# Graph kernel on one core: GpSimd waits for the landing of four gathers in the middle of each group of eight

## The chip, the cores and the metric

The kernel runs on one core of a Trainium2 chip. The metric is the device time of one execution in microseconds. Three runs of the kernel before gave 9080.73, 9087.52 and 9103.37 us; the median is 9087.52 us.

## What is computed

One node array x of 6250 rows by 256 goes through two layers. Each has a graph part and a mixture of experts part, all in float32. The reference, cut to its core:

```python
edge_index = jnp.stack([src, dst])          # 206250 edges, sorted by dst
x = x + _L0_gnn_ref(_layernorm(x, axis=-1), edge_index, ...)       # attention, 4 heads
x = x + _L0_ffn_ref(_layernorm(x, axis=-1)[None], ...)[0]          # 8 experts, top 2
x = x + _L1_gnn_ref(_layernorm(x, axis=-1), src, dst, edge_weight, ...)
x = x + _L1_ffn_ref(_layernorm(x, axis=-1)[None], ..., edge_index)[0]  # 4 experts

# in _L0_gnn_ref
e = jax.nn.leaky_relu(a_src[src] + a_dst[dst], negative_slope=NEG_SLOPE)
...
out = jax.ops.segment_sum(alpha[:, :, None] * h[src], dst, num_segments=N)

# in _L1_gnn_ref
messages = edge_val[:, None] * embeddings[edge_src]
neighbor_emb = jax.ops.segment_sum(messages, edge_dst, num_segments=embeddings.shape[0])
```

Both graph parts have the same skeleton: for every edge the row of its source node is fetched, scaled, and added to the sum of its destination node.

## The kernel before, in words

The 206250 sorted edges are cut into tiles of 128. `graph_pass` (L693) runs twice, once per graph part. Fetching the 128 source rows of a tile is one gather, an indirect DMA that GpSimd issues from a table in HBM to `G`, 128 rows of 1040 bytes in pass 1 and of 1024 bytes in pass 2. Gathers come in groups of `GRP` = 8, and `G` is a ring of `RINGS` = 4 groups. Each ring place r has its own semaphore `gather_done[r]`, which each gather raises by 16 when it has landed, 128 for a whole group.

**Pass 1** (`attend`, 208 groups, 1664 gathers, L831). GpSimd waits at the start of group k until the last pair of sums of group k - 4 is done, since it will write into the same ring place, and then issues eight gathers with nothing between them. The consumers of group k are:

- VectorE waits for `gather_done` (L789), forms the attention argument (`g_Z` L987, `g_L`, `g_ARG` L998), multiplies the rows by the factors in four products (L981), builds one-hot matrices (`g_S` L921) and adds the sums out of PSUM into `acc` (L944).
- ScalarE takes the exponentials (L1064, L1065) and copies the turned one-hots out of PSUM (`g_ST` L1048).
- TensorE turns the one-hots (L1095), spreads node values to edges (`g_pA` L1105) and sums messages by destination, two tiles to a pair and four pairs to a group (`g_pM` L1115). Each pair raises the semaphore `part` by one. ScalarE's copy, VectorE's adds and its `g_Z`, and GpSimd's next group all wait on values of `part`.

In step k TensorE's order is: turns for k + 1, pairs 2 and 3 of group k - 1, pair 0 of group k, the spread for k + 1, pair 1 of group k. From round 1 to round 50 of 52, VectorE and ScalarE also do a piece of a sort of other edges in every second group (L897 and L903, or L1052 and L1056). After the last group GpSimd issues 16 small scatters of that sort (L618).

**Pass 2** (202 groups, 1616 gathers, L839). A slot of work may straddle two groups, so ScalarE waits for the landed counts and raises `tiles` (L1040, L1041), TensorE waits on `tiles` and forms the sums (L1147) in two halves, each raising `sum`. VectorE builds one-hots times weight (L932) and adds to `acc` (L952), one of each in turn. SyncE waits for a number of `sum` from a table (L819) and raises `room`; GpSimd waits on `room` before group g, at most three groups ahead of what was consumed. In the last 130 groups one scatter (L618) follows the eight gathers.

Each engine's instructions are written out in program order in its own block; nothing is reordered. GpSimd has one instruction queue, so all that it issues stands in the order shown. The two steps in question, as they stand:

```python
if k >= RINGS:
    pool.wait_ge(s["part"], summed(k - RINGS, PAIRS - 1))      # pass 1
...
at_least(pool, s["room"], g - AHEAD + 1)                       # pass 2
```

`rounds0` is 0 for pass 1 and 52 for pass 2, the number of times that each ring place was filled before.

Of the kernel before, what the change touches and what calls it, by code (L numbers as in the profile page):

```python
# [47 lines left out]
GRP = 8  # L48
RINGS = 4
# [97 lines left out]
def at_least(eng, sem, value):  # L147

    if not isinstance(value, int) or value > 0:
        eng.wait_ge(sem, value)  # L150
# [542 lines left out]
def graph_pass(sh, tag, planned, planned_block, table, width, acc, acc_zeroed, gather_done, rounds0, keep=None, gmax=None,  # L693
# [11 lines left out]
    HG = GRP // 2  # L705
# [9 lines left out]
    with Scope(nc) as sc:  # L715
# [81 lines left out]
        def summed(k, pair):  # L797
            return k * PAIRS + 5 + pair
# [5 lines left out]
        @block.sync  # L804
        def _(sp):
            sp.dma_start(IDX[:, :], planned[0] if attend else src_tiles).then_inc(s["loaded"], 16)
            sp.dma_start(REL[:, :], planned[1]).then_inc(s["loaded"], 16)
            if attend:
                sp.dma_start(BLK[:, :], planned_block).then_inc(s["loaded"], 16)
            if ranking:  # L810
                sp.dma_start(DST, sort.dst_t).then_inc(s["loaded"], 16)
                sp.dma_start(SRC, sort.src_t).then_inc(s["loaded"], 16)
            if not attend:
                sp.dma_start(WT[:, :], planned[2]).then_inc(s["loaded"], 16)

                with sp.Fori(0, TG - AHEAD) as g:
                    sums = sp.value_load(tables.summed(g), min_val=1, max_val=2 * SG)
                    sp.wait_ge(s["sum"], sums)
                    sp.sem_inc(s["room"], 1)  # L819

        @block.gpsimd
        def _(pool):
            pool.wait_ge(s["loaded"], n_loads)

            def step_attending(k):

                r = k % RINGS
                if k >= RINGS:
                    pool.wait_ge(s["part"], summed(k - RINGS, PAIRS - 1))
                for u in range(GRP):  # L830
                    pool.indirect_dma_start(G[:, r, u, :], None, table, bass.IndirectOffsetOnAxis(  # L831
                        ap=IDX[:, k * GRP + u:k * GRP + u + 1].bitcast(U32), axis=0)).then_inc(gather_done[r], 16)

            def step_placing(g):

                r = g % RINGS
                at_least(pool, s["room"], g - AHEAD + 1)
                for u in range(GRP):
                    pool.indirect_dma_start(G[:, r, u, :], None, table, bass.IndirectOffsetOnAxis(  # L839
                        ap=IDX[:, g * GRP + u:g * GRP + u + 1].bitcast(U32), axis=0)).then_inc(gather_done[r], 16)  # L840
                if g >= TG - place:
                    sort.place(pool, 1)

            if attend:
                pool.iota(RANK, [[P, NTF]], base=P * NTS, channel_multiplier=1,
                          allow_small_or_imprecise_dtypes=True).then_inc(s["rank0"], 1)
                for k in range(SG):
                    step_attending(k)
                pool.wait_ge(s["prep"], 7)
                pool.wait_ge(s["addr"], 4)  # L850
                sort.place(pool, tail)
            else:
                for g in range(TG):
                    step_placing(g)
                sort.place(pool, tail)
# [1859 lines left out]
```

## Time and profile before

| | |
|---|---|
| median of 3 runs | 9087.52 us (9080.73 to 9103.37) |
| span of the profiled execution, first to last instruction | 9073.9 us |
| the profiled execution's own time | not listed apart; the median lies 13.6 us above its span |
| busy share: PE, DVE, ACT, POOL | 64%, 43%, 17%, 60% |
| gathers of pass 1, first to last start | 202.7 to 2756.2 us |
| gathers of pass 2, first to last start | 4301.8 to 6845.9 us |
| granted TensorE clock, mean | 0.756 |

The profile is of one execution. PE is TensorE, DVE is VectorE, ACT is ScalarE, POOL is GpSimd, SP is SyncE. A timeline row gives start, duration, engine, line, operation, output and inputs; in brackets stands the idle time of the engine before it and what ended it. "issue" there means that the engine waited for nothing the profile shows, "remote" that the releaser was found on no recorded instruction. An indirect DMA's busy time on POOL is the making of its descriptors, not the transfer.

### The profile page before, as it was taken

Reading aid. Unit: us, or ns where it says so; the run is one execution under the profiler, and the core shown is the slowest. Engines: PE = TensorE matmul, PEld = TensorE weight load, DVE = VectorE, ACT = ScalarE, POOL = GpSimd, SP = SyncE. Lnnn points to the kernel's source line nnn. Section 1 sums busy time; section 2 is a strip of 40 time slices with the busy share of each in tenths; the row PEclk is TensorE's granted clock in tenths of the full one; section 3 lists DMA queues with packets and bytes.
Section 4 is the critical chain, followed back from the end, with each engine's and each line's share of the span. In section 5 each row is a group of like instructions: output and inputs, shape, how many; then the busy total and the mean of one; then the engine's idle time right before and its main releaser. Section 6 shows DMA issues by size and latency. Waiting matters only on the chain. (4 is left out here: it accounts for less than half of the span.)

```text
span 9073.9 us, 116515 instructions
## 1 busy us (share of the span) xinstructions
PE 5819.2 (64%) x27644; PEld 4894.5 (54%) x27645; DVE 3938.2 (43%) x10109; ACT 1583.2 (17%) x3574; POOL 5476.3 (60%) x5690
## 2 busy tenths in 40 slices
PE   4677777777772488881444444444442579998984
PEld 3566665666662477771333333333331478888883
DVE  4566666777776400004444434434331532222225
ACT  1122222221220233330000000000000233333331
POOL 3566666666666466666666666666666246666662
PEclk7777777777775599995777777776765768888786
DMA  3333333333333144443333222222220022222345
GB/s 113 84 88 87 89 89 85 88 86 87 87 86 108 49 140 145 145 145 114 88 89 88 86 81 81 81 80 82 79 82 19 22 60 67 65 69 65 67 67 163
DMA packets 426058, 793.32 MB, mean 87 GB/s; under 512 B 129162, under 2 KB 267134, under 8 KB 425684
## 3 DMA queue, kind: packets, MB, share of 16 engines
q0 software_dynamic: 235504, 474.87, 21.0%
q1 hardware_dynamic: 190436, 317.20, 10.4%
q14 instruction: 84, 0.69, 0.0%
q8 instruction: 34, 0.56, 0.0%
HBM read 720.67 MB, written 70.98 MB: 87 GB/s over the span
## 5 line engine op out<-in xcount | busy, mean ns | idle before, releaser
L1147 PE MATMUL g_pM<-g_G,g_S 128*128 x3328 | 1178.4, 531 | 1570.5 <-DVE g_S L932 834.9
L831 POOL DMA_INDIRECT g_G<-table,X x1664 | 1620.8, 974 | 933.8 <-issue 447.1
L839 POOL DMA_INDIRECT g_G<-table,g_IDX x1616 | 1534.2, 949 | 863.9 <-issue 460.8
L1147 PEld LDWEIGHTS g_pM<-g_G,g_S 128*128 128x128 f32 x3328 | 903.1, 278 | 1845.8 <-issue 1652.9
L1115 PE MATMUL g_pM<-g_G,g_S 128*128 128x260 f32 x3328 | 1196.4, 499 | 593.1 <-DVE acc L944 555.7
L1691 POOL DMA_INDIRECT q_G<-table,slot x1072 | 1037.1, 967 | 591.5 <-issue 288.3
L618 POOL DMA_INDIRECT slots<-sort_PAIR,sort_ADDR x1024 | 1012.3, 989 | 521.4 <-issue 310.7
L952 DVE TENSOR_TENSOR acc<-g_pM,acc 128x256 f32 x1664 | 697.2, 419 | 1257.4 <-remote 693.1
L1115 PEld LDWEIGHTS g_pM<-g_G,g_S 128*128 128x128 f32 x3328 | 722.3, 238 | 906.4 <-DVE acc L944 647.2
L944 DVE TENSOR_TENSOR acc<-g_pM,acc 128x260 f32 x1664 | 711.4, 428 | 468.4 <-remote 204.0
L932 DVE TENSOR_SCALAR g_S<-iota,g_REL,g_WT 128x128 f32<-128x128 f32 x1664 | 588.8, 354 | 288.2 <-issue 259.2
L1105 PEld LDWEIGHTS g_pA<-keep,g_ST 128*128 128x128 f32 x3328 | 555.1, 257 | 80.7 <-issue 69.0
L1477 PE MATMUL q_pH<-ew_XT,ew_W 128*128 (+1 forms) x3136 | 552.6, 347 | 52.9 <-ACT ew_GT L1496 34.6
L1105 PE MATMUL g_pA<-keep,g_ST 128*128 x3328 | 550.1, 297 | 11.9 <-ACT g_ST L1048 1.2
L1477 PEld LDWEIGHTS q_pH<-ew_XT,ew_W 128*128 128x128 f32 x3136 | 514.4, 254 | 71.7 <-ACT ew_GT L1496 42.3
L981 DVE TENSOR_TENSOR g_G<-g_G,g_pF 128x512 f32<-128x512 f32 x832 | 546.6, 678 | 0.3 <-issue 0.3
L1351 ACT ACTIVATE f_XT<-f_pT 128x512 f32<-128x512 f32 x49 | 28.9, 596 | 2804.9 <-issue 2640.8
L2372 PE MATMUL e_pH<-e_XT,e_W 128*128 128x128 f32 x3360 | 410.9, 282 | 164.4 <-ACT e_XT L2316 155.3
L2372 PEld LDWEIGHTS e_pH<-e_XT,e_W 128*128 128x128 f32 x3360 | 391.9, 195 | 204.9 <-ACT e_GT L2333 178.7
L2350 DVE TENSOR_TENSOR e_Y<-e_pY,ew_B 128x256 f32<-128x256 f32 x105 | 44.6, 425 | 924.8 <-PE e_pY L2381 895.2
L1487 PE MATMUL q_pY<-ew_W,ew_GT 128*128 128x256 f32 x1568 | 435.9, 428 | 0.0
L2381 PE MATMUL e_pY<-ew_W,e_GT 128*128 x1680 | 380.3, 379 | 0.7 <-DVE e_Y L2350 0.7
(335 smaller groups left out, 7007.3 us busy)
## 6 DMA issues: line engine op xcount, KB each, us to landing
e_W<-in_L_ffn_W SPq DMA_DIRECT2D x210, 512.0 KB
sort_PAIR<-slot_rows SPq DMA_DIRECT2D x66, 512.0 KB
g_G<-table,X POOLq DMA_INDIRECT x1664
g_G<-table,g_IDX POOLq DMA_INDIRECT x1616
ys_all<-ew_Y SPq DMA_DIRECT2D x196, 128.0 KB
sm_Y<-ys_all SPq DMA_DIRECT2D x28, 896.0 KB, 10.5
q_ST<-slot_rows SPq DMA_DIRECT2D x34, 512.0 KB
sort_ADDR<-slot_rows SPq DMA_DIRECT2D x34, 512.0 KB
```

The costliest lines, as they stand in the source:

```text
L618: pool.indirect_dma_start(self.slots, bass.IndirectOffsetOnAxis(ap=self.ADDR[:, t:t + 1].bitcast(U32), axis=0), self.PAIR[:, t, :], None). ...
L831: pool.indirect_dma_start(G[:, r, u, :], None, table, bass.IndirectOffsetOnAxis(ap=IDX[:, k * GRP + u:k * GRP + u + 1].bitcast(U32), axis= ...
L839: pool.indirect_dma_start(G[:, r, u, :], None, table, bass.IndirectOffsetOnAxis(ap=IDX[:, g * GRP + u:g * GRP + u + 1].bitcast(U32), axis= ...
L932: v.tensor_scalar(S[:, r, u, :], sh.iota[:, :], rel, WT[:, bass.ds(k * GRP + u, 1)], ALU.is_equal, ALU.mult).then_inc(s["onehot"], 1)
L944: v.tensor_tensor(node_sums(blk), pM[u % BANKS][:, 0:width], node_sums(blk), ALU.add).then_inc(s["added"], 1)
L952: v.tensor_tensor(node_sums(blk), pM[r % 2 * 2 + u // HG][:, u % HG, :], node_sums(blk), ALU.add).then_inc(s["added"], 1)
L1105: m = pe.matmul(pA[:, r % 2, u, :], ST[:, u, :], nodes, start=True, stop=True)
L1115: m = pe.matmul(pM[u % BANKS][:, 0:width], S[:, r, u, :], G[:, r, u, :], start=True, stop=True)
L1147: m = pe.matmul(pM[r % 2 * 2 + half][:, u % HG, :], S[:, r, u, :], rows.rearrange("p a d -> p (a d)"), start=True, stop=True)
L1477: m = pe.matmul(self.pH[e % n][:, c, :], self.W1[:, e, k, c * P:(c + 1) * P], self.XT[:, bass.ds(i, 1), k, :].rearrange("p a m -> p (a m)" ...
L1691: pool.indirect_dma_start(G[:, r, u, :], None, table, bass.IndirectOffsetOnAxis(ap=node_of_slot[:, 2 * (k * GRP + u):2 * (k * GRP + u) + 1 ...
L2372: m = pe.matmul(pH[j % 2][:, c, :], W1[:, j, k, c * P:(c + 1) * P], XT[:, j % 2, k, :], start=(k == 0), stop=(k == KC - 1))
```

## The change

Behind the fourth gather of each group, in both passes, GpSimd now waits on the semaphore of the group's ring place until the 64 increments of these four gathers have arrived on top of all those of earlier rounds. `HG` is `GRP // 2` = 4. Nothing else is changed, and no instruction is moved.

```diff
@@ step_attending(k), pass 1
                 for u in range(GRP):
                     pool.indirect_dma_start(G[:, r, u, :], None, table, bass.IndirectOffsetOnAxis(
                         ap=IDX[:, k * GRP + u:k * GRP + u + 1].bitcast(U32), axis=0)).then_inc(gather_done[r], 16)
+                    if u == HG - 1:
+                        pool.wait_ge(gather_done[r], (k // RINGS + rounds0) * 16 * GRP + 16 * HG)
@@ step_placing(g), pass 2
                 for u in range(GRP):
                     pool.indirect_dma_start(G[:, r, u, :], None, table, bass.IndirectOffsetOnAxis(
                         ap=IDX[:, g * GRP + u:g * GRP + u + 1].bitcast(U32), axis=0)).then_inc(gather_done[r], 16)
+                    if u == HG - 1:
+                        pool.wait_ge(gather_done[r], (g // RINGS + rounds0) * 16 * GRP + 16 * HG)
                 if g >= TG - place:
                     sort.place(pool, 1)
```

## Rows read from the trace of the kernel before

**Rows 1.** The page, part 1: busy time and share of each engine.

```profile
PE 5819.2 (64%) x27644; PEld 4894.5 (54%) x27645; DVE 3938.2 (43%) x10109; ACT 1583.2 (17%) x3574; POOL 5476.3 (60%) x5690
```

**Rows 2.** Busy time in two windows, pass 1 and pass 2, in the page's order.

```profile
202.70:2757.10 2554.40, 1968.97 (x8236) 1543.45 (x8236) 1711.90 (x3607) 506.88 (x869) 1620.78 (x1664) 0.76 0.32 87
4301.80:6846.90 2545.10, 1168.07 (x3296) 895.12 (x3296) 1034.05 (x3295) 0.00 (x0) 1662.28 (x1745) 0.71 0.29 83
```

**Rows 3.** Waits of POOL in pass 1: us in total, times, longest.

```profile
POOL g_G L831 <- issue: 447.1, 1460, 0.5
POOL g_G L831 <- PE g_pM L1115: 363.7, 143, 10.9
POOL g_G L831 <- remote: 122.9, 61, 2.1
```

**Rows 4.** Waits of POOL in pass 2, the same columns.

```profile
POOL g_G L839 <- issue: 460.8, 1505, 1.3
POOL g_G L839 <- SPq L819: 382.7, 110, 11.5
POOL slots L618 <- issue: 39.3, 129, 0.3
```

**Rows 5.** Line L831: who waited for its gathers (us, times), the whole answer.

```profile
who waited for it (us, times):
  DVE g_Z L987: 7.6, 1
```

**Rows 6.** Timeline of POOL in pass 1: first and eighth gather of a group, next starts.

```profile
904.89 0.94 POOL L831 DMA_INDIRECT g_G<-table,X  x1 [2.77 <-PE g_pM L1115]
...
913.64 0.95 POOL L831 DMA_INDIRECT g_G<-table,X  x1 [0.30 <-issue]
...
916.62 0.94 POOL L831 DMA_INDIRECT g_G<-table,X  x1 [2.03 <-PE g_pM L1115]
...
929.48 0.94 POOL L831 DMA_INDIRECT g_G<-table,X  x1 [3.17 <-PE g_pM L1115]
```

**Rows 7.** The other engines at the end of that group.

```profile
912.20 3.24 PE L1115 MATMUL g_pM<-g_G,g_S 128*128 128x260 f32 x8 [2.05 <-DVE acc L944]
...
916.32 1.02 ACT L1048 ACTIVATE g_ST<-g_pT 128x1024 f32<-128x1024 f32 x1 [4.27 <-PE g_pM L1115]
916.52 1.00 DVE L944 TENSOR_TENSOR acc<-g_pM,acc 128x260 f32 x2 [2.64 <-PE g_pM L1115]
```

**Rows 8.** Timeline of the start of pass 1, 32 gathers without a wait.

```profile
211.54 0.95 POOL L831 DMA_INDIRECT g_G<-table,X  x1 [0.30 <-issue]
...
214.41 0.19 DVE L987 TENSOR_TENSOR g_Z<-g_G,g_pA 128x32 f32<-128x32 f32 x1 [7.65 <-DMA g_G<-table,X]
...
221.49 2.08 PE L1115 MATMUL g_pM<-g_G,g_S 128*128 128x260 f32 x4
...
241.54 0.95 POOL L831 DMA_INDIRECT g_G<-table,X  x1 [0.30 <-issue]
...
247.66 0.19 DVE L987 TENSOR_TENSOR g_Z<-g_G,g_pA 128x32 f32<-128x32 f32 x1 [27.89 <-remote]
```

**Rows 9.** Timeline of pass 2, two groups of gathers with two scatters.

```profile
5405.08 0.97 POOL L839 DMA_INDIRECT g_G<-table,g_IDX  x1 [3.40 <-SPq L819]
...
5414.88 0.33 DVE L932 TENSOR_SCALAR g_S<-iota,g_REL,g_WT 128x128 f32<-128x128 f32 x1
...
5429.80 0.35 DVE L932 TENSOR_SCALAR g_S<-iota,g_REL,g_WT 128x128 f32<-128x128 f32 x1 [0.97 <-issue]
...
5430.91 0.97 POOL L839 DMA_INDIRECT g_G<-table,g_IDX  x1 [3.44 <-SPq L819]
```

**Rows 10.** Timeline of the end of pass 1; the last of the 16 scatters is first.

```profile
2776.43 0.95 POOL L618 DMA_INDIRECT slots<-sort_PAIR,sort_ADDR  x1 [0.30 <-issue]
...
2781.29 0.19 DVE L987 TENSOR_TENSOR g_Z<-g_G,g_pA 128x32 f32<-128x32 f32 x1 [18.81 <-remote]
...
2790.43 0.19 DVE L987 TENSOR_TENSOR g_Z<-g_G,g_pA 128x32 f32<-128x32 f32 x1 [1.34 <-PE g_pM L1115]
```

## The prediction

> **What bounds the kernel now.** I read busy shares first, then the two passes by window, then who waits for whom, then single groups in time. The shares name no engine: PE has 64%, POOL 60% [rows 1]. The passes are 5100 of 9074 us, and in them POOL issues 1664 gathers in 2554 us and 1616 gathers plus 129 scatters in 2545 us, with no other engine above 1970 us busy [rows 2]. So the question is how POOL's time per group is made up.
>
> A gather costs POOL 0.95 us (mean 0.974 in pass 1) and 0.306 us of issue behind it (447.1 / 1460) [rows 2, 3], so gathers start 1.25 us apart. Eight are 10.0 us. A group takes more: 11.7 us from 904.89 to 916.62 and 12.9 us to 929.48 [rows 6]. The rest is the wait at the group's start, 204 waits in pass 1 with 486.6 us in all, mean 2.39 [rows 3], and 110 in pass 2 with 382.7 us, mean 3.48 [rows 4]. In pass 2 only every second group waits: from 5405.08 to 5430.91 eighteen indirect DMAs stand in one stream [rows 9].
>
> Nobody waits for the gathers' data: one wait of 7.6 us, the first of the pass [rows 5]. So the ring is full, POOL waits for its consumers, and a landing is needed by nobody for two groups.
>
> But these consumers are not simply slow. At 912.20 PE starts pairs 2 and 3 of a group. By the row it is done at 915.44 for both, so the first pair should be free some 1.5 us earlier, yet ScalarE's copy and VectorE's add, which wait for that first pair alone, start at 916.32 and 916.52 [rows 7]. The eighth gather had ended issuing at 914.59 (913.64 + 0.95) [rows 6], so this is 1.7 to 1.9 us after the end of issue. How long after issue do gathers land? The very first group says it: the eighth gather ends issuing at 212.49, and `g_Z`, which waits only for the landing, starts at 214.41, 1.92 us later [rows 8]. The consumers go on just as the gathers in flight have landed. At the pass's start this is plain: 32 gathers run without a wait until 242.49. The pair sums that PE finishes at 223.57 free `g_Z` of the next group, whose rows have landed long ago, and it starts at 247.66 [rows 8]. That is 24 us held, and released only after the stream has stopped. At the end of the pass the 16 scatters do the same: VectorE idles 18.8 us until their stream is over, and then does a whole group in 9.1 us (2781.29 to 2790.43) [rows 10]. In pass 2, one-hots follow at once early in a stream and with 0.97 us of "issue" between them late in it [rows 9].
>
> My reading: **news from PE, and late in a long stream the other engines' instructions too, are held up while GpSimd streams indirect DMAs, and are let go when those in flight have landed.** The present boundary wait is a lock: POOL waits for a pair sum, and that is held until POOL has been still for about 2 us.
>
> **The change part by part.** It adds 208 + 202 = 410 waits and removes nothing. Queued behind each on POOL are the group's gathers 5 to 8, in late pass 2 one scatter, and then the next group's boundary wait.
>
> *A mid wait.* No row has this wait, so it is bounded. Below: 1.92 us from end of issue to a consumer's start [rows 8]. Above: 3.44 us, the wait behind a stream of eighteen [rows 9]. I take 2.05: its stream is eight gathers long, and the waits behind such a stream are 2.03 [rows 6] and "remote" 122.9 / 61 = 2.01 [rows 3]. It replaces one issue gap of 0.306, so it adds 1.744 us, 410 times: 208 x 1.744 = 363 us and 202 x 1.744 = 352 us.
>
> The Trainium skill, DMA: Bandwidth & Descriptors, Anatomy of one DMA, gives 2.0 us plus bytes / 436e3 for a GpSimd DMA, setup included. An estimate by it is 2.3 us from issue for 133 KB, thus 1.36 us of waiting behind the 0.95 us, and the sum would be 410 x 0.69 = 283 us less than mine. The trace has 2.87 us for this length (211.54 to 214.41) and decides [rows 8].
>
> *The boundary wait.* It hides the mid wait if it goes away. Between two mid waits stand again eight gathers (four of this group, four of the next), so once per period everything held is let go. PE's pair sum that the boundary asks for is four groups old; consumers need 9.1 us for a group when let run [rows 10], the new period is 10.0 + 1.74 = 11.8 us, so they draw ahead until they wait for data. Then the boundary costs nothing: pass 1 loses its excess of 486.6 - 204 x 0.306 = 424 us, pass 2 its 382.7 - 110 x 0.306 = 349 us. A few remain where consumers do extra work, of up to 10.9 us [rows 3] and 11.5 us [rows 4]; I leave 12 us in pass 1 and 12 us in pass 2.
>
> *Ends of the passes.* At the end of pass 1 consumers now have over two groups left, held behind the scatters and done at 9.1 us each [rows 10]. With consumers ahead, one group less is left: 9 us, in pass 2 about 6 us (a bit less work per group). What is late next is the landing of gathers 5 to 8, which `g_Z` waits for.
>
> **Sum.** Pass 1: 363 - 424 + 12 - 9 = -58. Pass 2: 352 - 349 + 12 - 6 = +9. Together -49 us against the profiled span: 9073.9 - 49 = 9025. The median stands 13.6 us above that span, so 9038. In pass 2 nearly nothing is won, since one wait of 3.5 per two groups is traded for two of 2.05; in pass 1 one of 2.39 for one of 2.05.
>
> All other work (projections, experts, slot pass) is untouched.
>
> **Rivals.** (a) *The boundary waits stay and the mid waits come on top.* POOL is on the path, a landing is exposed, and 410 x 1.744 = 715 us are added: 9800 us. The mechanism: POOL's period grows from 11.7 to 13.5 us and the pair sum is still not told when POOL comes to the boundary. It decides from the point where over one group in seven keeps a second stop (49 / 1.744 = 28 groups of 208 in pass 1 cancel the gain; 44 of them lose 0.3%). For it: groups with a sorting piece run late, the wait before 929.48 is 3.17 us [rows 6], and one that misses the mid stop may be held for a whole period. Against it: each second stop lets the consumers go twice in a period, and they have 13.5 us for 9.1 us of work, so they catch up and the second stop goes. A share of a third of the groups, 70 + 67 stops of 1.744 = 239 us above the sum, is the most I can believe: 9277 us. The Trainium skill's rule for overlap (DMA: Bandwidth & Descriptors, Rules for kernel authors) says to issue early and wait on the semaphore late; by it this rival would be the whole story.
>
> (b) *Nothing changes within 0.3%* (27 us, about what a measurement of this kernel can tell). The limit is how fast held news can be passed on, so that a group needs 12.2 us however the stops are cut, or the mid wait is 2.2 us instead of 2.05 (410 x 0.15 = 61 us more) and eats the gain. For it: pass 1 and pass 2 take the same time per group today, 12.3 and 12.6 us, with quite different work. 9087, range 9060 to 9115.
>
> (c) *A larger gain.* The mid wait is at its lower bound 1.92 (-53 us), no long waits remain (-24), and both pass ends give back what stream stops hide today (another -20): 8941 us. For it: the 24 us stall at the start of pass 1 and the 18.8 us at its end [rows 8, 10].
>
> (d) *The wait does nothing*, because the four gathers have landed when POOL comes to it. Excluded: POOL comes to it at the end of issue of the fourth, 1.92 us too early.
>
> **How the numbers follow.** The forecast with its own range 8990 to 9060 has 0.45, (c) 0.13, (b) 0.22, (a) 0.20, mostly in its mild form. The likeliest time is 9038. The range runs from (c)'s middle, 8965, to 9180, which takes in 54 groups in both passes that keep a second stop above (b)'s 9087 (93 / 1.744); about 0.05 is left out below and 0.12 above. Faster by over 0.3%: 0.45 + 0.13 = 0.58. Within: 0.22. Slower: 0.20.
>
> **What the changed profile would show.** Right: before the fifth gather of every group POOL idles about 2.05 us, released by the gather's own DMA, 410 times; the waits of POOL on PE L1115 and on SyncE's L819 fall from 487 and 383 us to some tens; the first gather to the last takes about 2504 us in pass 1 and 2560 us in pass 2; `g_Z` now waits for DMA; VectorE in pass 2 runs at its early pace nearly throughout. ScalarE's copy in pass 1 starts about 1.8 us after the fourth gather's end of issue instead of the eighth's. Wrong: waits on PE L1115 remain about 200 in number (rival a), or the mid wait is 2.2 us or more (b). If the mid wait leaves held news held, my reading of the lock is wrong as a whole, and the time lies above 9180.

## The result, and the profile after

The changed kernel takes 8955.41 us (median of 3 runs, 8952.56 to 8956.40) against 9087.52 us: a ratio of 0.9854 with a 95% interval of 0.9836 to 0.9871, 132 us less. I had forecast 49 us less, 9038 us, with a range down to 8965. The direction and the exchange of waits hold, the size does not. The profiled execution has a span of 8954.6 us against 9073.9 us, 119.3 us less. The other 13 us are spread between executions: in every run on record the time is 1.7 to 2.1 us above the span of the same execution, so the profiled execution of before took about 9076 us, less than any of the three timed ones, while the profiled one of after took 8956.4 us, 1 us above the median.

First the page, part 1, of the changed kernel, and its row for line L831 (busy us, mean ns, then idle time in front of it and what ended most of it).

```profile
PE 5685.7 (63%) x27644; PEld 4815.9 (54%) x27645; DVE 3949.8 (44%) x10109; ACT 1585.0 (18%) x3574; POOL 5436.7 (61%) x5690
...
L831 POOL DMA_INDIRECT g_G<-table,X x1664 | 1576.4, 947 | 876.9 <-DMA g_G<-table,X 433.4
```

The shares again name nobody. Then the two passes by window, in the page's order of engines, each from its first to the end of its last gather:

```profile
210.40:2663.60 2453.20, 1800.73 (x8279) 1440.60 (x8280) 1729.86 (x3628) 509.53 (x873) 1576.42 (x1664) 0.80 0.33 90
4193.00:6743.00 2550.00, 1208.62 (x3312) 925.12 (x3312) 1038.60 (x3320) 0.00 (x0) 1663.93 (x1745) 0.71 0.28 83
```

Pass 1 is 101 us shorter, pass 2 is 5 us longer [rows 2]. The granted TensorE clock of pass 1 is 0.80 instead of 0.76 in these rows; POOL does not wait for PE in this pass any more, and no run separates what part the clock has in that. And POOL's waits (us in total, times, longest), first in pass 1, then in pass 2:

```profile
POOL g_G L831 <- DMA g_G<-table,X: 433.4, 208, 2.8
POOL g_G L831 <- issue: 428.2, 1406, 0.3
...
POOL g_G L831 <- PE g_pM L1119: 15.2, 50, 0.3
```

```profile
POOL g_G L841 <- issue: 433.6, 1414, 3.1
POOL g_G L841 <- DMA g_G<-table,g_IDX: 412.8, 201, 2.4
POOL slots L618 <- issue: 39.9, 131, 0.3
```

This is the exchange that was forecast, and it is complete on this chip. The mid wait is there 208 and 201 times, 2.08 and 2.05 us each (the 202nd, 3.1 us, stands under "issue"). The waits at the group boundary, 486.6 us in pass 1 [rows 3] and 382.7 us in pass 2 [rows 4], are gone to the last: the 50 that still name PE last 0.30 us each, as an ordinary issue gap does, and SyncE, whose count released them in pass 2, is named no more. POOL's time in pass 1 now adds up without a rest: 1576.4 + 428.2 + 15.2 + 433.4 = 2453.2 us.

The timeline of one group in pass 1 (start, duration, engine, line, operation; in brackets the idle time before):

```profile
906.66 0.95 POOL L831 DMA_INDIRECT g_G<-table,X  x1 [0.30 <-PE g_pM L1119]
...
910.42 0.95 POOL L831 DMA_INDIRECT g_G<-table,X  x1 [0.30 <-issue]
...
912.98 0.19 DVE L991 TENSOR_TENSOR g_Z<-g_G,g_pA 128x32 f32<-128x32 f32 x1 [3.10 <-remote]
...
913.41 0.95 POOL L831 DMA_INDIRECT g_G<-table,X  x1 [2.05 <-DMA g_G<-table,X]
...
918.42 0.95 POOL L831 DMA_INDIRECT g_G<-table,X  x1 [0.30 <-issue]
```

From 906.66 to 918.42 the group takes 11.76 us, where before it took 11.7 to 12.9 [rows 6]. `g_Z`, for which VectorE had been idle, starts 1.6 us after the fourth gather's end of issue (911.37): the consumers are let go in the middle of the group now. The trace also holds the times at which semaphores rise, and "news from PE" here is a rise of `part`. Over gathers 200 to 1650, PE's first news in each of the 181 mid stops comes 1.74 us (median) after the fourth gather's end of issue (5% to 95%: 1.64 to 1.81); before, it came 1.72 us (median) after the eighth's. An example from before: the pairs whose matmuls end at 913.63 and 915.44 by their rows raise `part` at 916.30 and 916.36. Not all news in a stream is held: in the kernel before, the next rise of `part` follows the end of a pair by 0.01 us (median of 88) when the pair ends in the first 2 us of a stream, and by 3.75 us (median of 80) when it ends 6 to 8 us into it.

Pass 2, two groups with a scatter in each:

```profile
5309.88 0.94 POOL L841 DMA_INDIRECT g_G<-table,g_IDX  x1 [2.04 <-DMA g_G<-table,g_IDX]
...
5312.50 0.35 DVE L936 TENSOR_SCALAR g_S<-iota,g_REL,g_WT 128x128 f32<-128x128 f32 x1 [0.67 <-issue]
...
5337.07 0.94 POOL L841 DMA_INDIRECT g_G<-table,g_IDX  x1 [2.07 <-DMA g_G<-table,g_IDX]
```

Where a stream of eighteen ran between two waits [rows 9], there is now a stop in each nine. And the end of pass 1:

```profile
2658.90 0.94 POOL L831 DMA_INDIRECT g_G<-table,X  x1 [2.51 <-DMA g_G<-table,X]
...
2673.76 0.19 DVE L991 TENSOR_TENSOR g_Z<-g_G,g_pA 128x32 f32<-128x32 f32 x1 [8.59 <-remote]
...
2695.20 0.36 DVE L1206 TENSOR_TENSOR f_Z<-keep 128x196 f32<-128x196 f32 x1 [0.53 <-PEq L135]
```

VectorE is held for 8.6 us behind the sixteen scatters, not for 18.8 [rows 10], and the work behind the pass (`f_Z`) starts 32.6 us after the last gather's start, not 46.3.

Stage by stage, the spans differ by: start of pass 1 +7.7 us (POOL waits 80.6 us for the load of `fsrc`, not 71.7; kernels with the same code there show 71 to 81), pass 1 -101.3, its end -13.7, between the passes -1.2, pass 2 +4.8, its end -6.8, the stage behind it -8.4, the rest -0.3. Sum -119.2.

**A part that was not in the forecast.** Gathers in pass 1 last 947 ns in the mean, not 974 [rows 2]: 44.4 us of POOL's busy time. The rows show which. Before, where VectorE ranks for the sort:

```profile
1528.38 2.34 DVE L897 TENSOR_TENSOR_SCAN X<-g_pF,g_BASE,X 128x1024 f32<-128x1024 f32 x1
...
1529.87 0.94 POOL L831 DMA_INDIRECT g_G<-table,X  x1 [0.30 <-issue]
...
1530.89 1.35 DVE L903 COPY_PREDICATED X<-X 128x1024 f32<-128x1024 int32 x1 [0.16 <-DVE X L897]
...
1531.11 1.91 POOL L831 DMA_INDIRECT g_G<-table,X  x1 [0.30 <-issue]
```

The gather beside the predicated copy takes 1.91 us; the gather beside the scan takes 0.94. There are 50 such copies, all of them 6.02 us behind the start of a stream, and 53 gathers above 1.05 us; the 50 beside the copies start 0.21 to 0.40 us into the copy. After, the copy starts 8.7 to 10.1 us behind the stream's start. Sixteen copies stand in no gather, as here:

```profile
1522.83 0.95 POOL L831 DMA_INDIRECT g_G<-table,X  x1 [0.31 <-issue]
...
1524.18 1.36 DVE L907 COPY_PREDICATED X<-X 128x1024 f32<-128x1024 int32 x1 [0.16 <-DVE X L901]
...
1525.82 0.94 POOL L831 DMA_INDIRECT g_G<-table,X  x1 [2.05 <-DMA g_G<-table,X]
```

### The profile page after: what moved, and what is told of

Same layout as the page of the kernel before. It is cut to its first block and busy times, and to the rows that moved or that the text cites. A ratio compares the mean times of both kernels' runs of the same rounds, so it can differ in the third digit from the quotient of the medians.

```text
span 8954.6 us, 116515 instructions
## 1 busy us (share of the span) xinstructions
PE 5685.7 (63%) x27644; PEld 4815.9 (54%) x27645; DVE 3949.8 (44%) x10109; ACT 1585.0 (18%) x3574; POOL 5436.7 (61%) x5690
## 5 line engine op out<-in xcount | busy, mean ns | idle before, releaser
L1151 PE MATMUL g_pM<-g_G,g_S 128*128 x3328 | 1213.9, 543 | 1525.6 <-ACTq L1045 1372.6
L831 POOL DMA_INDIRECT g_G<-table,X x1664 | 1576.4, 947 | 876.9 <-DMA g_G<-table,X 433.4
L1151 PEld LDWEIGHTS g_pM<-g_G,g_S 128*128 128x128 f32 x3328 | 929.2, 287 | 1810.3 <-issue 1608.0
L1119 PE MATMUL g_pM<-g_G,g_S 128*128 128x260 f32 x3328 | 1249.2, 534 | 661.4 <-DVE acc L948 638.4
L1119 PEld LDWEIGHTS g_pM<-g_G,g_S 128*128 128x128 f32 x3328 | 817.7, 263 | 947.6 <-DVE acc L948 726.2
L618 POOL DMA_INDIRECT slots<-sort_PAIR,sort_ADDR x1024 | 1017.5, 994 | 487.1 <-issue 310.6
L1109 PEld LDWEIGHTS g_pA<-keep,g_ST 128*128 128x128 f32 x3328 | 426.6, 202 | 55.1 <-issue 36.9
L1109 PE MATMUL g_pA<-keep,g_ST 128*128 x3328 | 410.0, 255 | 6.1 <-ACT g_ST L1052 1.2
```

The lines of the kernel that those rows point to most:

```text
L618: pool.indirect_dma_start(self.slots, bass.IndirectOffsetOnAxis(ap=self.ADDR[:, t:t + 1].bitcast(U32), axis=0), self.PAIR[:, t, :], None). ...
L1109: m = pe.matmul(pA[:, r % 2, u, :], ST[:, u, :], nodes, start=True, stop=True)
L1119: m = pe.matmul(pM[u % BANKS][:, 0:width], S[:, r, u, :], G[:, r, u, :], start=True, stop=True)
L1151: m = pe.matmul(pM[r % 2 * 2 + half][:, u % HG, :], S[:, r, u, :], rows.rearrange("p a d -> p (a d)"), start=True, stop=True)
```

## The experiments

The chips differ (the kernel before takes 9074 to 9211 us on them), so ratios to the kernel before on the same chip are compared, and stages within one chip where nothing else is said. `no_stop`, at 0.9997, stands for the kernel before where I compare stages on its chip. A profile is of one execution: three traces from one chip with the same code in pass 1 (`pass1_only`, `change_again`, `late_stops16`) have 2492 to 2502 us for it, so a stage is known to about 10 us.

**1. The halves of the change.** The wait of one pass is left out in each.

```diff
 # pass1_only: step_placing without
-                    if u == HG - 1:
-                        pool.wait_ge(gather_done[r], (g // RINGS + rounds0) * 16 * GRP + 16 * HG)
 # pass2_only: step_attending without the same two lines (with k)
```

> The mid wait in pass 1 alone. Lock theory (held news is let go when GpSimd stops for a landing): pass 1 shrinks by about 101 us and its tail by 15, as in the trace of the change, the rest stays: 9087 - 116 = 8971 us. If pass 2 carried half of the gain: 9020 us.

> The mid wait in pass 2 alone. Lock theory: one wait of 3.5 us per two groups is traded for two of 2.06, so the pass itself costs 5 us more and its tail gives 16 back: 9087 - 11 = 9076 us, within 0.3%. If pass 2 carried half of the gain: 9020 us.

Measured: 0.9873 (0.9843 to 0.9903) and 0.9979 (0.9966 to 0.9992). Both came as the lock theory had them (8971 of 9087 is 0.9872, and pass 2 alone within 0.3%). The product is 0.9852, the change 0.9854, so the halves add and nearly all is won in pass 1. By stages against `no_stop`, pass 1 goes from 2606 to 2493 us with its wait, and pass 2 from 2562 to 2552 us with its own, a difference of the size of the spread; the end of pass 2 from 29 to 20 us.

**2. The wait, or the stop?** The wait stays as an instruction in its place, but on the group before, which has landed long ago.

```diff
-                    if u == HG - 1:
-                        pool.wait_ge(gather_done[r], (k // RINGS + rounds0) * 16 * GRP + 16 * HG)
+                    if u == HG - 1 and k > 0:
+                        pool.wait_ge(gather_done[(k - 1) % RINGS], ((k - 1) // RINGS + rounds0 + 1) * 16 * GRP)
```

> The wait stands at the same place, but for the eight gathers of the group before, the last of which was issued 5 us earlier and has landed: GpSimd runs through a wait and does not stop. Lock theory: no stop, nothing is let go, the boundary waits return: 9087 us, same as before. Rival (the wait as such, or fewer gathers that could be in flight, does it): faster by over 50 us.

Measured: 0.9997 (0.9981 to 1.0013). Its waits of POOL in pass 1:

```profile
POOL g_G L831 <- PE g_pM L1119: 472.6, 169, 10.6
POOL g_G L831 <- issue: 447.1, 1460, 0.5
POOL g_G L831 <- remote: 73.3, 35, 2.2
```

All 204 boundary waits are back, 545.9 us (this chip is one of the slower ones). A wait instruction that does not stop POOL does nothing here; the stop is what acts.

**3. Where the stop stands, and how many.**

```diff
 # behind_eighth
-                    if u == HG - 1:
+                    if u == GRP - 1:        # value: the whole group
 # fourth_and_eighth
+                    if u in (HG - 1, GRP - 1):
 # every_second
+                    if u == HG - 1 and k % 2 == 0:
```

> The same wait, but behind the eighth gather, where the boundary wait stands. Streams are again eight long and each group has one stop: if only the number of stops and the length of streams matter, the same time as the change within 0.3%, 1.3% faster than before in pass 1's share, with waits of 2.08 us. If the place matters (a pair sum that comes just behind the stop must wait for the next), the waits on part come back at 0.5 us a group and the gain halves.

> Waits behind the fourth and behind the eighth gather. The boundary needs no second stop, so it is pure cost: 410 x (2.08 - 0.31) = 726 us above the change, 9680 us. If shorter streams (four instead of eight) also sped the consumers so that GpSimd was no longer the bound, it would cost less than 600 us.

> The mid wait in even groups only, so that streams are sixteen gathers long. Lock theory: half the mid waits are saved (205 x 1.78 = 364 us), but news is held for some 10 us of each 22 us; with 9.1 us of work per group the consumers have too little time, boundary waits return, and pass 1 takes as long as before or a little more: 0 to 2% slower than the change. Rival (8 gathers per stop is more than needed): 2 to 4% faster than the change.

Measured: 0.9892 (0.9871 to 0.9913); 1.0615 (1.0583 to 1.0648); 1.0211 (1.0191 to 1.0231). The place is of little weight in the passes: behind the eighth, pass 1 takes 2456 us and pass 2 2556 us, 4 and 7 us more than the change's 2452 and 2549. The whole kernel is 0.4% slower than with the stop behind the fourth, a little outside the 0.3% that was expected; of the 29 us between the spans 16 lie behind the first gather of the slot pass (`q_G`), and why was not settled. A second stop in each group adds its full price, since there is no boundary wait left for it to replace:

```profile
POOL g_G L831 <- DMA g_G<-table,X: 781.6, 374, 2.9
POOL g_G L831 <- issue: 382.2, 1247, 0.5
POOL g_G L831 <- PE g_pM L1119: 85.3, 41, 2.1
```

These are 415 stops of 2.09 us (781.6 + 85.3 over 374 + 41). On the same chip, against the kernels with one stop per group, pass 1 takes 365 us more (2858 against 2493 of `pass1_only`) and pass 2 354 us more (2906 against 2552 of `pass2_only`), together 719 us beside the 726 expected. Over the kernel before the run lies 570 us. A stop in every second group is worse than none: streams of sixteen form, and the 147 boundary waits that are left take 427 us (339.8 + 87.3) beside 217 us of stops. It is 3.6% slower than the change, where 0 to 2% was expected. Rival (a) exists, then, in this kernel and not in the change.

**4. Must POOL wait for the landing?** Iotas into a tile of their own stand in place of the wait. They need no transfer and stop the stream for 0.75, 1.26, 1.77 or 2.27 us (1, 2, 3 or 4 of them).

```diff
-                        pool.wait_ge(gather_done[r], (k // RINGS + rounds0) * 16 * GRP + 16 * HG)
+                        if k > 0:
+                            pool.wait_ge(s["filled"], k * n)
+                        for f in range(n):
+                            pool.iota(FILL[:, f, :], [[1, 512]], base=0, channel_multiplier=0,
+                                      allow_small_or_imprecise_dtypes=True).then_inc(s["filled"], 1)
```

> In place of the wait, GpSimd writes 512 numbers a partition into a scratch buffer (iota, some 0.5 to 0.6 us and one issue gap), so the stream pauses for less than 1 us and no landing is waited for. Lock theory: a pause shorter than the 1.9 us to the landing lets nothing go; the boundary waits stay, partly shortened by the filler's time: between 0 and 3% slower than before. Rival (any pause in descriptor making lets the news through): boundary waits gone, 410 x 1 us less than the change, some 3% faster than before.

> Four such fillers, some 3 to 3.6 us without a new gather and no wait on a landing. Lock theory: the gathers in flight land during them, held news goes, and the boundary waits are gone or nearly so; the pause itself is about 1.3 us longer than the wait of 2.08 us: 410 x 1.3 = 533 us above the change, about 4% slower than before. Rival (the wait on the semaphore itself is what helps): boundary waits of 486 and 383 us stay on top, over 10% slower than before.

> Nothing is left out. In both passes the wait behind the fourth gather is replaced by two iotas of GpSimd into a tile of their own, so the pause between the fourth and the fifth gather is about 1.26 us (0.75 us with one iota, 2.27 us with four, by their runs) and waits for no transfer. Theory 'landing' (news is let go when the gathers in flight have landed, which takes about 1.8 us from the last one's issue): 1.26 us is too short, the boundary waits stay near one iota's (median 1.5 us) or near before's 2.03 us, and the time is 9240 to 9290 us. Theory 'backlog' (the news is worked off during any pause, and a group of eight needs some 1.7 to 2.0 us of pause in all, in one piece or in several): the median boundary wait is near 1.0 us and the time stays near one iota's, 9150 to 9200 us; pass 1 then takes about 2540 us as with no pause and with one iota.

> Nothing is left out. Three iotas in place of the wait: a pause of about 1.77 us (estimate from 0.75 us with one and 2.27 us with four). Both theories allow that the boundary waits go; the point is how much pause is enough. If 1.77 us is enough: 208 pauses in pass 1 and 202 in pass 2, each 0.31 us shorter than the change's 2.08 us, take 127 us off the change's 8955 us: 8830 us, with all boundary waits at 0.30 us. Theory 'landing' with its 1.8 us from issue to landing: just short of it, boundary waits stay in a good part of the groups, 9000 to 9300 us. Theory 'backlog': boundary waits of 0.3 to 0.6 us at most, 8830 to 8950 us.

Measured, with readings of the semaphore events of gathers 200 to 1650 (181 pauses; one can also be without news because PE has none to tell):

| pause, us | ratio (interval) | pauses without news from PE, of 181 | boundary waits of pass 1, us |
|---|---|---|---|
| 0.30 (`no_stop`) | 0.9997 (0.9981 to 1.0013) | not counted | 545.9 |
| 0.75 (`filler1`) | 1.0115 (1.0095 to 1.0135) | 164 | 400.7 |
| 1.26 (`filler2`) | 1.0248 (1.0206 to 1.0291) | 117 | 608.7 |
| 1.77 (`filler3`) | 1.0037 (1.0023 to 1.0051) | 87 | 283.2 |
| 2.27 (`filler4`) | 1.0005 (0.9996 to 1.0015) | none | 62.1 (0.30 each) |
| 2.08 (the change) | 0.9854 (0.9836 to 0.9871) | none | 62.2 (0.30 each) |

The rows come from chips on which the kernel before takes 9205 us (`no_stop`), 9211 us (`filler2`, `filler3`) and 9081 to 9088 us (the others; 486.6 us of boundary waits in the kernel before there, not 545.9). Read by pass, the table is not one curve. With one iota pass 1 takes 2541 us, about as before (2553), and all of the loss is in pass 2, 2662 us instead of 2544. With two it is the other way round: pass 1 takes 2832 us (2606 in `no_stop`), pass 2 2562 us, the same as in `no_stop`. POOL's waits on PE in pass 1 with two, three and four iotas:

```profile
POOL g_G L832 <- PE g_pM L1128: 579.0, 125, 8.3
```

```profile
POOL g_G L832 <- PE g_pM L1128: 258.9, 128, 6.6
```

```profile
POOL g_G L832 <- PE g_pM L1128: 28.0, 92, 0.3
```

A pause of 2.27 us with no wait on a transfer clears the boundary as the wait does. Its time is the change's plus the longer pause: 208 x 0.19 + 202 x 0.28 (means 2.27 and 2.34 against 2.08 and 2.06) = 96 us of the 119 us between their spans. (The 4% that was expected came from a pause of 3 to 3.6 us; the four iotas took 2.27.) With a pause of 1.77 us about half of the groups get no news, and this is best seen in time (three iotas, two groups):

```profile
1003.65 1.60 POOL L838 IOTA g_FILL<- 128x512 f32 x3
...
1004.66 0.19 DVE L1000 TENSOR_TENSOR g_Z<-g_G,g_pA 128x32 f32<-128x32 f32 x1 [2.14 <-remote]
...
1015.15 1.59 POOL L838 IOTA g_FILL<- 128x512 f32 x3
...
1016.91 0.96 POOL L832 DMA_INDIRECT g_G<-table,X  x1 [0.16 <-issue]
...
1019.07 0.19 DVE L1000 TENSOR_TENSOR g_Z<-g_G,g_pA 128x32 f32<-128x32 f32 x1 [5.58 <-remote]
...
1024.84 0.95 POOL L832 DMA_INDIRECT g_G<-table,X  x1 [3.21 <-PE g_pM L1128]
```

The first pause lets `g_Z` start; in the second nothing starts, VectorE idles 5.58 us, and POOL pays 3.21 us at the boundary. The boundary waits of this run mostly alternate in the first half of the pass, 0.3 and 2.1 to 3.4 us. With two iotas it is worse. VectorE (its waits from 500 to 2500 us) is held for up to 9.4 us. My reading, not shown apart, is that PE's sums are then really late, not only told late; POOL's waits for them sum to more than with no iota:

```profile
DVE g_Z L1000 <- remote: 500.6, 93, 9.4
```

Neither theory of `filler2` and `filler3` is right as a whole. "Backlog" had them at 9150 to 9200 and 8830 to 8950 us; by their ratios, on a chip with 9081 us for the kernel before, they take 9306 and 9115 us. "Landing" had 9240 to 9290 and 9000 to 9300, so it is nearer. But with one iota the news at the boundary came 1.28 us (median) after the end of issue, before the last transfer's end, which is at 1.48 us in this kernel as in the four others where I read it (before, after, two and three iotas). It came 0.44 us earlier than before's 1.72, about what the iota had lengthened the mid pause by (0.45 us). So the last transfer's end is not what lets the news go, though it comes near in time. Nor is there one delay: where news comes in a pause of two or three iotas, it comes 0.99 and 1.00 us (medians) after the end of issue, not 1.74 as in the change or 1.73 as with four iotas. Some pauses without news had nothing to tell (by the ends of the pairs some 15 of the 87 with three iotas). What lets the news go was not settled; shown is that a pause of 2.08 us let news out 181 times in 181, and one of 1.77 us in about half.

**5. The copies beside the gathers.** The predicated copy is cut to 16 of its 1024 columns, in the kernel before and in the changed one. Both kernels leave out most ranks of the sorted edges with it, so the second expert layer works on other data.

```diff
-                v.copy_predicated(RANK, EQ[j].bitcast(I32), SCAN).then_inc(s["rank"], 1)
+                v.copy_predicated(RANK[:, 0:16], EQ[j].bitcast(I32)[:, 0:16], SCAN[:, 0:16]).then_inc(s["rank"], 1)
```

> The kernel before with VectorE's predicated copies of the sort (50 of 1.35 us, L903) cut to 16 of 1024 columns, so the ranks of the sorted edges are left out and the second expert layer's graph is not the reference's. The trace of before shows 50 gathers of about 1.9 instead of 0.95 us beside these copies. If these 47 us were on the path: about 50 us faster than before (0.5%), gathers at 0.947 us mean. If the boundary wait swallows them: under 15 us.

> The changed kernel with the same cut copies. Its gathers are at 0.947 us already, GpSimd is the bound and not VectorE: within 10 us of the change. Rival (VectorE's load in sorting groups still counts): 30 to 60 us faster than the change.

Measured: 1.0016 (1.0003 to 1.0030) and 0.9918 (0.9902 to 0.9935). In the kernel before the gathers of pass 1 fall from 974 to 948 ns, as expected of the collision, yet POOL's waits rise:

```profile
POOL g_G L831 <- issue: 447.7, 1461, 0.5
POOL g_G L831 <- PE g_pM L1115: 407.3, 148, 10.8
POOL g_G L831 <- remote: 108.9, 55, 2.1
```

The boundary takes 516 us, not 487 [rows 3], and of 42.7 us less busy time only 12.6 us reach pass 1 (2540.9 us). With narrow copies the change gains 83 us in pass 1 (2457.7), with the full ones 101: so some 18 of the 101 us come with the collisions, and the other 26 of the 44 us in the busy row only took the place of waiting. These are differences of single traces, so the split into 18 and 26 is rough. By the medians the change is worth 92 us here (9089.5 to 8997.4). Neither run came out as expected as a whole: `narrow_before` is 15 us slower than before, not faster, and `narrow_after` some 56 us slower than the change (0.9918 against 0.9854), not within 10. By the traces 26 and 32 us of this lie behind pass 2, where the other data go; traces with the right data differ there by up to 29 us as well, so only the rows of pass 1 are used.

**6. The same stop elsewhere.** GpSimd's long streams of scatters (L618) got a stop behind each eighth, in the changed kernel (`scatter_stops8`), in the kernel before (`scatter_stops_before`), and then only from scatter 841 on, behind pass 2 (`late_stops`, with each sixteenth `late_stops16`).

```diff
                 ap=self.ADDR[:, t:t + 1].bitcast(U32), axis=0), self.PAIR[:, t, :], None).then_inc(self.s_placed[j], 16)
+            if count > 1 and t >= 841 and t % 8 == 8 - 1:        # without t >= 841 in the first two
+                pool.wait_ge(self.s_placed[j], (t // (2 * GRP) * GRP + t % GRP + 1) * 16)
```

> The changed kernel, and in every row of more than one scatter of the sort GpSimd also waits behind each eighth until it has landed. Lock theory: stages that stream 15 to 110 scatters beside other work get their news earlier (ScalarE and VectorE idle up to 29.5 us at once in the node stage after pass 2): 20 to 80 us faster than the change. If these stages are bound by GpSimd's scatters themselves: some 900 / 8 x 1.8 = 200 us slower at most.

> The kernel before with the stops in the scatters alone. Same gain or loss as they bring to the changed kernel, plus up to 15 us at the end of pass 1, where VectorE idles 18.8 us behind 16 scatters.

> Nothing is left out. The changed kernel, and in the streams of scatters behind pass 2 (from scatter 841 on) GpSimd also waits behind each eighth scatter until its two halves' latest have landed. With such stops in all long streams of scatters the stage behind pass 2 came down from 438 to 327 us and the stage between the passes went up from 1498 to 1562 us. The theory that a pause helps where other engines' work or their news is needed late in a stream, and costs where the stream itself is the bound: the first is kept, the second is left away, so 8955 less 111 = 8845 us (8830 to 8865). The rival, that the gain behind pass 2 depends on what the earlier stops did: 8955 us, no change against the changed kernel.

> Nothing is left out. The late stops of scatters and the three iotas together. If both parts act and 1.77 us of pause is enough: 8830 less 111 = 8720 us. If 1.77 us is not enough: the time of the three iotas alone less about 111 us, which says that the two parts add.

> Nothing is left out. As late_stops, with a stop behind each sixteenth late scatter in place of each eighth. The stops of each eighth cut one wait of 131 us in the stage behind pass 2 (GpSimd for the data of its next scatters) to 35 us. Theory: what matters is that the streams are broken before they hold the other engines' news for long; streams of 16 hold it up to twice as long, so a good part of the 131 us comes back: the stage takes 380 to 430 us (353 with each eighth, 438 with none) and the ratio is 0.978 to 0.984. Rival: any few pauses are enough; the stage then takes 340 to 355 us and the ratio is near that of late_stops, 0.9745 or a little less.

> The changed kernel as it is, on the same chip as the run beside it, so that this is compared directly. Expected 0.9854 of the kernel before, within 0.9835 to 0.9875; by its parts (0.9873 with the pause in pass 1 alone, 0.9979 with it in pass 2 alone) 0.9852.

Measured: `scatter_stops8` 0.9827 (0.9810 to 0.9843), `scatter_stops_before` 0.9959 (0.9944 to 0.9973), `late_stops` 0.9745 (0.9727 to 0.9764), `late_stops_filler3` 0.9919 (0.9892 to 0.9945), `late_stops16` 0.9824 (0.9811 to 0.9838), and the changed kernel again 0.9844 (0.9827 to 0.9862). The up to 15 us that were expected at the end of pass 1 in `scatter_stops_before` did not come: the stop behind the eighth of those sixteen scatters lasts 1.42 us, and VectorE still idles 17.45 us, after 18.81 us before [rows 10].

Against `narrow_after` on the same chip, stops in all scatters take the stage behind pass 2 from 441 to 327 us and the stage between the passes from 1497 to 1562 us, where the stream itself is the bound. Kept behind pass 2 alone they give the lowest ratio here, `late_stops`. One wait of POOL there tells why (131.3 us in the profile of the changed kernel, whose chip had neither run). First `filler3` and `late_stops`, which share a chip, then `change_again` and `late_stops16`, which share another; `filler3` and `change_again` have no stops in this stage:

```profile
POOL slots L618 <- PEq L135: 143.0, 1, 143.0
```

```profile
POOL slots L618 <- DMA slots<-sort_PAIR,sort_ADDR: 37.5, 22, 5.6
POOL slots L618 <- PEq L135: 34.9, 1, 34.9
```

```profile
POOL slots L618 <- PEq L135: 144.3, 1, 144.3
```

```profile
POOL slots L618 <- PEq L135: 130.6, 1, 130.6
...
POOL slots L618 <- DMA slots<-sort_PAIR,sort_ADDR: 19.0, 11, 5.0
```

L135 is the end of a block of instructions, where every engine waits for the others. In this block POOL streams 110 scatters while PE, VectorE and ScalarE compute the node rows in seven rounds, which start with `f_XR`. Counted from the last gather, the stream of `change_again` runs from 21 to 160 us, and VectorE's first `f_XR` of the first three rounds start at 27, 32 and 186 us: two rounds get in early, the third only behind the stream, and POOL then waits for the rest. In `late_stops` the rounds start at 28, 33, 67, 92, 115, 140 and 161 us. Stops of each eighth cut the wait from 143 to 35 us, for 22 stops with 37.5 us in all (1.7 us each in the mean), and the stage takes 353 us (447 in `filler3`). The ratio is what was expected (0.9745 x 9087.5 = 8856 us). Stops of each sixteenth cut little: the third round starts at 182 us, the wait is 130.6 us instead of 144.3, 14 us less for 19.0 us of stops, and the stage takes 443 us (449 in `change_again`), more than the 380 to 430 expected. The ratio, 0.9824, lies in the expected range, but cannot be told from the 0.9844 of `change_again`: the intervals overlap.

The change again, on a slower chip (9211 us for the kernel before), confirms its ratio. The boundary is not wholly free there: 8 waits above 1 us with 49.9 us in all are left in pass 1, the longest 4.0 us, and 3 to 5 such waits with 37 to 46 us in `pass1_only`, `late_stops` and `late_stops16`, all on slower chips. Three iotas with late stops are 0.9919 against 1.0037 without, so the late stops add as much to a bad pause as to a good one (0.0118, against 0.0099 from `change_again` to `late_stops`).

## Why the prediction was wrong

**Right: what bounds the passes.** POOL's stream plus the boundary wait was the bound. With both in the sum, all of pass 1 is accounted for.

**Right: the lock.** News from PE that comes a few us into a stream is held while GpSimd streams, and is let go in a stop that is long enough. `no_stop`, `filler4` and the 1.74 us show it. The words "when those in flight have landed" go too far, as `filler1` shows, and what does let it go stays open.

**Right: the mid wait.** Taken at 2.05 us, measured 2.08 and 2.06 (201 at 2.05, one at 3.1): 7 and 2 us more than in the sum. The rule of the Trainium skill (DMA: Bandwidth & Descriptors, Anatomy of one DMA), 2.0 us and the bytes' time, would have put it at an estimated 1.36 us. Measured, 0.95 + 2.08 = 3.03 us pass from the start of issue until POOL goes on.

**Wrong: the size.** The forecast was 9025 for the span and 9038 for the time. The span came out 70 us lower, the time 83 us. Term by term:

- *Pass 1, "363 - 424 + 12".* Forecast -49, measured -101.3. The failed step is the first line of the forecast's argument, "a gather costs POOL 0.95 us (mean 0.974 in pass 1)": I saw the two numbers, and let the sum go by waits alone, as if the 0.974 stayed. 44.4 us of the 52 us miss are there by POOL's busy time. The mean hid 50 gathers of 1.9 us, all in the second half of the pass and at one phase of the stream, 6.02 us; a change that shifts the consumers by half a group was bound to move that phase. The narrow copies say that only some 18 us of it are a gain in their own right: without the collisions, the waits at the boundary would have been 30 us longer, and the change takes those as well. So the miss is mostly of one row, but its cause has two halves. The other 8 us are the residual waits below, 12 us, less the 7 us of the mid wait, and a rest of 3 us.
- *The residual waits, 12 + 12.* Measured 0 on this chip, and 37 to 50 us in pass 1 in four profiles on slower ones, so the 0 is partly luck. I left them for groups with sorting work, whose waits ran up to 10.9 us.
- *Pass 2, "352 - 349 + 12".* Forecast +15, measured +5: the residual again.
- *The ends.* Forecast -9 and -6, measured -13.7 and -6.8.
- *"All other work is untouched".* The stage behind pass 2 is 8 us shorter and the start 8 us longer, the latter by the load.
- *The 13.6 us between span and median.* I carried them over to the changed kernel as if they belonged to it. They were the spread between executions, and 0.8 us there: 12.8 of the 83 us.

**The rivals.** The time falls nearest to (c), 8941, but not for (c)'s reasons. Of these, the mid wait at its lower bound (-53) did not come, the missing long waits (-24) did, and the ends gave 5 us of the 20. Rival (a) did not occur. It was the one that went with the Trainium skill's advice to wait late (DMA: Bandwidth & Descriptors, Rules for kernel authors): by it each early wait is a loss, 715 us in the prediction's sum, and 132 us were gained. The advice holds where nothing else depends on the pause, as the second stop per group of `fourth_and_eighth` shows (719 us in the two passes), and it misleads where the pause itself does the work. (b), a 2.2 us mid wait or 12.2 us for a group however the stops are cut, is excluded by the 2.08 us and by the 2453 us, 11.8 us for a group of pass 1.

**The range.** Its lower end was (c)'s middle, 8965, and the result is 10 us below. With a 0.13 chance on a case, its middle is no end: that case's lower half belonged in it.

## What to carry to other kernels

When GpSimd streams indirect DMAs and another engine's finished work seems to be noticed only at the stream's end, compare the end of that work with the start of what waits for it. In this kernel a stop of about 2 us in each eight or nine DMAs cost less than it gave back, and it can do so if a wait of the same size is already being paid, or if other engines must work beside a long stream; where neither is so, it costs its full length. A pause that was too short or too rare was worse than none here. And a mean duration that is 3% above the usual one is worth a look at its slow members before it is carried over to a changed kernel.

## What the runs showed of the hardware that I had not expected

- PE's news from late in a stream waits for a pause, and short pauses often let none out: with 2.08 us news came in 181 of 181 cases, with 1.77 us in 94, with 1.26 us in 64, with 0.75 us in 17, while the last transfer had ended after 1.48 us. It is not a fixed length: in the scatters stops of 1.7 us in the mean were enough for the other engines to go on.
- Late in a stream the other engines' own register instructions are slow. In pass 2 of the kernel before, those of ScalarE that start 15 to 20 us into a stream take 0.70 us (median of 157), those in its first 5 us 0.15 us (705). With a stop in each group no stream is that long.
- A predicated copy of VectorE over 128 x 1024 elements (1.35 us) doubles the descriptor making of a gather that starts 0.21 to 0.40 us into it, 0.95 to 1.91 us, 50 times of 50. It does not slow one that was under way (9 before, 32 after), and the scan in front of it slows none of the 100 gathers that start beside it.
- Most of the same collision was free as long as POOL waited at the boundary: 42.7 us less busy time gave 12.6 us in pass 1.
- A stop behind each sixteenth scatter cuts a wait of 144 us only to 131; a stop behind each eighth cuts one of 143 us to 35.
